# Tile order and an early merge in the routed layer of a small vision tower: expert tiles by their place within an expert, two groups' results merged beside the last tiles

## The reference, cut to what matters

```python
shared_out = _expert(x, sg, su, sd)              # silu(x @ g.T) * (x @ u.T) @ d.T, 704 hidden
probs = softmax(x @ wr.T + rb)                    # 7 routed experts
scores, idx = top_k(probs, 2)
scores = scores / scores.sum(-1, keepdims=True)
w = sum(scores[..., None] * one_hot(idx, 7), -2)
out = shared_out
for e in range(7):
    out = out + w[..., e:e+1] * _expert(x, rg[e], ru[e], rd[e])
# then block 1: layernorm, attention with 16 heads, layernorm, feed-forward
```

## Time and profile before

| | us |
|---|---|
| three runs, median (lowest to highest) | 1051.48 (1050.4 to 1051.73) |
| the profiled execution, own time | 1051.63 |
| its span, first to last instruction | 1049.8 |
| PE busy in the span | 971.6 (93%) |
| DVE, ACT, POOL busy | 709.0, 660.5, 359.1 |

### The profile page before, as it was taken

The page is one execution under the profiler, slowest core; times in us unless marked ns, Lnnn a source line. Parts: engine busy times, 40 slices in busy tenths (PEclk is TensorE's granted clock), DMA queues, the critical chain, the costliest instruction groups (busy, mean ns, idle before and its releaser), DMA issues.

```text
span 1049.8 us, 29183 instructions
## 1 busy us (share of the span) xinstructions
PE 971.6 (93%) x10745; PEld 892.2 (85%) x10746; DVE 709.0 (68%) x1393; ACT 660.5 (63%) x1206; POOL 359.1 (34%) x285
## 2 busy tenths in 40 slices
PE   4979999989999987999999999997899999799998
PEld 4967888868888886999999999996678888699998
DVE  3536677675556566899999999992566777655443
ACT  3337677855465635687777777772567678555652
POOL 0253454465665650111111111113545554611210
PEclk9999999989999998999999999999889999999999
DMA  6720000009211135111111111104311100000000
GB/s 231 240 96 3 2 3 3 3 7 357 41 35 31 40 75 221 35 36 40 35 35 40 40 35 35 40 30 141 81 26 26 26 3 4 2 13 12 24 25 24
DMA packets 30974, 57.67 MB, mean 55 GB/s; under 512 B 13202, under 2 KB 22418, under 8 KB 29724
## 3 DMA queue, kind: packets, MB, share of 16 engines
q1 hardware_dynamic: 15696, 38.38, 11.5%
q0 software_dynamic: 13664, 15.25, 4.8%
q10 hardware_dynamic: 1516, 2.65, 0.7%
HBM read 41.47 MB, written 14.67 MB: 53 GB/s over the span
## 4 chain that ended last, share of the span: by engine, by line
PE 72%; DVE 9%; ACT 9%; issue 5%; DMA 3%; POOL 1%; SPq 0%; DVEq 0%; ACTq 0%; POOLq 0%
PE ps L1400 19%; PE ps L1405 15%; PE ps L1407 14%; PE ps L1406 14%; PE ps L1805 3%; PE ps L1549 3%; PE ps L1538 2%; DVE Hd L1149 2%; DMA x_in<-in_xT_dram 2%; ACT L817 1%; ACT Hf_hi L811 1%; PE ps L1703 1%; ACT Sg L817 1%; DVE hsum L1139 1%; ACT L831 1%
## 5 line engine op out<-in xcount | busy, mean ns | idle before, releaser
L1303 DVE TENSOR_TENSOR tile_w<-arena,tile_w 128x704 fp32r<-128x704 f32 x129 | 142.7, 1134 | 26.9 <-ACT tile_w L880 24.2
L559 POOL DMA_INDIRECT routed_out<-yt,tile_to x43 | 42.1, 979 | 275.6 <-DVE yt L1321 271.5
L880 ACT ACTIVATE tile_w<-arena 128x704 fp32r x129 | 122.3, 984 | 1.4 <-issue 1.4
L1405 PE MATMUL ps<-tile_w,xTs 128*128 128x352 f32 x344 | 115.3, 335 | 4.5 <-DVE h L1276 3.0
L1406 PE MATMUL ps<-tile_w,xTs 128*128 128x352 f32 x344 | 111.6, 324 | 0.0
L1407 PE MATMUL ps<-tile_w,xTs 128*128 128x352 f32 x344 | 111.5, 324 | 0.0
L429 POOL TENSOR_TENSOR Km<-KT,cst 128x592 f32<-128x592 f32 x64 | 75.7, 1184 | 68.9 <-PE ps L1400 42.1
L1149 DVE TENSOR_TENSOR Hd<-Sg,ps 128x296 f32<-128x296 f32 x96 | 44.2, 461 | 81.2 <-ACT Sg L817 77.1
L811 ACT ACTIVATE Hf_hi<-Hd 128x296 fp32r<-128x296 f32 x96 | 43.3, 452 | 85.6 <-DVE Hd L1149 83.4
L1405 PE MATMUL ps<-xf_hi,gu_lo 128*128 128x296 f32 x272 | 85.8, 316 | 4.1 <-DVE Hd L1149 3.7
L1015 DVE SCALAR_TENSOR_TENSOR ps<-ps,bias 128x592 f32<-128x592 f32 x64 | 50.1, 782 | 53.0 <-PE ps L1400 53.0
(11 more groups left out here) (216 smaller groups left out, 3097.7 us busy)
## 6 DMA issues: line engine op xcount, KB each, us to landing
arena<-in_ew_dram SPq DMA_DIRECT2D x5, 2176.0 KB
x_in<-in_xT_dram SPq DMA_DIRECT2D x7, 888.0 KB, 5.4
xt<-routed_in SPq DMA_DIRECT2D x43, 129.0 KB, 2.0
arena<-in_ew_dram POOLq DMA_DIRECT2D x2, 2176.0 KB, 11.9
yg<-routed_out SPq DMA_DIRECT2D x8, 512.0 KB
out_dram<-h SPq DMA_DIRECT2D x8, 296.0 KB, 2.7
routed_in<-zero_x SPq DMA_DIRECT2D x12, 129.0 KB
qkv_w<-in_qkv_dram ACTq DMA_DIRECT2D x2, 768.0 KB, 6.2
```

What stands on the lines that cost most here:

```text
L880: act.activation(tile_w[half][0][:, cols], gate_up_of(w, half)[:, cols], ACT.Copy).then_inc(s.wh, 1)
L1303: dve.tensor_tensor(tile_w[half][1][:, cols], gate_up_of(w, half)[:, cols], tile_w[half][0][:, cols].bitcast(F32), ALU.subtract).then_inc( ...
L1405: pe.matmul(out_, w[1], x[0], start=start, stop=False)
```

## The change

Six things change together.

- **Tile order.** The table now puts tile k of every expert (its "level") ahead of tile k + 1 of any. It is computed on 43 partitions, one per tile, in more but narrower DVE instructions, with one PE product in the middle (`level_row`) and three that turn the columns into rows at the end. TABLE_AT spreads the pieces over chunks 0, 2, 3 and 4 (two) of group 6 and chunk 0 of group 7.
- **Early merge.** WHOLE says that the rows of group 0 are all in the first 21 tiles and those of groups 0 and 1 in the first 35. SP loads group 0 after `stored` 21 and group 1 after `stored` 35, GpSimd adds the two rows of each token between two stores, and in steps 25, 26, 39 and 40 PE transposes and DVE adds one half of the features (ADDS).
- **Norm of group 0** runs beside the last tiles: mean and variance on PE in the last step and ahead of the last down product, `cen` in DVE's last step, squares, the table switch and `lnv`, `rsd` on ACT, `xn` after DVE's last copy.
- **Weights.** The projection weights of block 1 are loaded by SP after step 40, no longer by ACT after tile 0; their lower half is computed by DVE, not by GpSimd.
- **Start of attention(1).** 8 products that nobody reads, not 22; groups 2 and 3 are loaded after the last tile; GpSimd adds group 2 after the split of group 1.
- **Start of the tiles and routing.** The table entries of tile 0 are read in chunk 3 of group 7; the first tile's transpose moves from chunk 3 to chunk 4; and DVE's `norm(r + 1)` moves from place 4 to the end of place 3.

```diff
+ADDS = {25: (0, 0), 26: (0, 1), 39: (1, 0), 40: (1, 1)}
+WHOLE = [EXPERTS * -(-(g + 1) * N // P) for g in range(2)]
...
+            t = 1
+            for adding in (25, 39):
+                with eng.Fori(0, (adding - t) // 2) as i:
+                    for k in range(2):
+                        step(2 * i + t + k, (t + k) % 2, i + (t + 1) // 2, None, False)
+                for t in range(adding, adding + 2):
+                    step(t, t % 2, (t + 1) // 2, ADDS[t], False)
+                t += 1
+            for t in range(t, TILES):
+                step(t, t % 2, (t + 1) // 2, None, t == TILES - 1)
...
+            for g, until in enumerate((24, 38)):
...
+                next_load(until, 0)
+                if g == 1:
+                    sp.wait_ge(C.mm1, FREE + 1)
+                sp.wait_ge(E.stored, FREE + WHOLE[g])
+                load_routed(g, g, yg_early)
+                next_load(until + 1, 1)
...
+            sp.wait_ge(C.mm1, FREE + 2)
+            sp.dma_start(qkv_w1, qkv1).then_inc(s_attw, 16)
+            sp.dma_start(out_w1, wo1).then_inc(s_attw, 16)
...
+                for g, until in enumerate((22, 36)):
+                    with pool.Fori(t // 2, until // 2) as i:
+                        for b in range(2):
+                            store(2 * i + b, b)
+                    sum_early(g)
+                    t = until
...
                 lower_x(a, 1, 1, xa[1])
+                if l == 1:
+                    sum_routed(2, 0, 1)
                 km(a, 0, 2)
...
                     if at == 4:
-                        if r + 1 < GROUPS:
-                            norm(r + 1)
                         slots_of(r, r % 2)
                     next(routes[r])
+                    if at == 3 and r + 1 < GROUPS:
+                        norm(r + 1)
...
+                        if l == 0 and g == GROUPS - 2 and j == 1:
+                            pe.wait_ge(s_t, TABLE_OPS[0])
+                            pe.wait_ge(s.r, RCHAIN * GROUPS)
+                            mm(ps[0:TILES, 6, 0:KT_MAX + 1], ones[0:KT_MAX, 0:TILES], level_row).then_inc(s.cnt_mm, 1)
+                        if l == 0 and g == GROUPS - 2 and j == 5:
+                            pe.wait_ge(s_t, TABLE_OPS[1])
...
-                        if l == 0 and last and j == 3:
+                        if l == 0 and last and j == 4:
                             pe.wait_ge(s.r, RCHAIN * GROUPS)
                             tile_in(0, 0, 0)
...
+                    if add:
+                        routed_out(yg_early, *add, 6)
                     hidden_t(t - 1, 1 - b)
                     gate_up_half(t, b, 1)
+                    if add:
+                        pe.wait_ge(C.h, 2 * add[0] + add[1] + 1)
                     if not last:
                         tile_in(t + 1, 1 - b, turn_next)
+                    else:
+                        mean(A[1], 0, 6)
                     tile_out(t - 1, w_before)
...
                 hidden_t(TILES - 1, 0)
+                pe.wait_ge(A[1].cen, FREE + 1)
+                variance(A[1], 0, 6)
                 tile_out(TILES - 1, weights_of(pe, TILES - 1))
...
+                over_tiles(act, step)
                 upper_down(TILES - 1)
+                squares(A[1], 0)
                 hidden_t(TILES - 1)
+                act.preload_act_table_set("natural_log_exp_and_others")
+                deviation(A[1], 0, 6)
```

More of the change, by code:

```diff
@@ L389, in _ @@
             load(0, 0)
             load(1, 1)
[L391 to L402 removed]
+            t = 2
@@ L880, in upper_weights, with step @@
                         act.activation(tile_w[half][0][:, cols], gate_up_of(w, half)[:, cols], ACT.Copy).then_inc(s.wh, 1)
-                def step(t, b, last):
+                def step(t, b, turn, add, last):
                     upper_down(t - 1)
@@ L1251, in step @@
                             routing(*routing_at(g, j))
-                        if l == 0 and g == GROUPS - 2 and j < TABLE_PIECES:
+                        if l == 0 and g == GROUPS - 2:
+                            for _ in range(TABLE_AT[j]):
+                                next(pieces)
+                        if l == 0 and last and j == 0:
                             next(pieces)
@@ L1483, in keep_going, with routed_out @@
                     mm(ps[:, 0, 0:2 * P], ident, cst[:, 0:2 * P])
+            def routed_out(of, g, c, bk):
+                pe.wait_ge(C.sum, g + 1)
+                for p in range(PAIRS):
+                    ins = pe.transpose(ps[:, bk, p * W2:(p + 1) * W2], of[:, p, 0, c * P:(c + 1) * P],
+                                       ident[0:W2, 0:W2])
+                ins.then_inc((C.mm0, C.mm1)[c], 1)
             def attention(l):
```

282 lines of the change are left out of this document (155 added, 127 removed).

## The result

| | before | after |
|---|---|---|
| runs beside each other, median (lowest to highest), us | 1050.94 (1049.59 to 1051.73, 4 runs) | 1034.80 (1031.88 to 1040.36, 4 runs) |
| the profiled execution, own time | 1051.63 | 1035.61 |
| its span | 1049.8 | 1033.8 |
| mean granted TensorE clock | 0.975 | 0.981 |

The ratio is 0.9845, 95% interval 0.9812 to 0.9878: faster by 16 us. Forecast were 1033.2 us, 8 in 10 between 1026.5 and 1042.

What follows compares the result with a forecast made beforehand. The prediction took PE's own work in the tiles and the 24 us handover into block 1 as the bound. Terms -12.7 + 2.0 - 4.5 - 3.1 = -18.3 gave 1033.2 us, 8 in 10 between 1026.5 and 1042.

Steps and rivals of the forecast that it cites:

- the likeliest case: Whole kernel: the forecast itself, terms summing to -18.3 us, 1033.2 us, own range 1030 to 1038; chance 0.52.
- The handover, -12.7: Last tile to attention(1): first projection 17 us earlier, PE standing 5 us for group 2's sum, 0.5 us half clock; -12.7 us.
- The tiles, +2.0: Tile steps: merge transposes on PE 1.5 us in all, plus 0.5 for code written out and two loops; +2.0 us.
- the sum of 2.38 is done early in step 24: Tiles: GpSimd's early sum of group 0 takes 2.38 us, in time for its use in step 25.
- Routing, -4.5: Routing: norm leaves DVE's chain (4.1 us) and PE's waits for it (6.3 us) go; -4.5 taken, between the two.
- The first rival: "Only the handover pays": routing waits pass to Hd, tile 2's rows stay late; -11.1 us, 1040.5; chance 0.18.
- The table, +0.55: Group 6 to tile 0: table wait +2.1, transpose -0.6, table entries read ahead -0.95; tile 0 starts 0.55 us late.
- Tile 2, -3.65 without what is ahead of it: Tile 2: rows land earlier without the weights' megabyte; wait -1.95, slow products -1.2 and -0.5; term -3.1 with the 0.55.
- Only the handover pays: Rival: routing waits pass to Hd and tile 2's rows stay late; -11.1 us, 1040.5; chance 0.18.
- More than the sum: Rival: waits that go take their half clock too; routing -6.5, start -4.5, handover -14.5; -24 us, 1027.5; chance 0.18.
- The handover is given back: Rival: group 2's sum waits for loads of groups 2 and 3, turn 0 stands 4 us more; 1044; chance 0.08.
- the slow GpSimd queue: Rival "slower than before": early loads over 24 us delay GpSimd's sums and stores, so tiles stand; 1055; chance 0.03.

Runs made afterwards that it cites:

- e3_hold_clock: Changed kernel plus 24 products that nobody reads on PE ahead of the merge of group 2 in turn 0; ratio 0.9858 to the kernel before.
- b3_loops_split: Kernel before, with only the tiles' steps laid out as in the change (two loops, six steps written out); 1051.65 us, one execution.
- e4_no_early_sum: Changed kernel with GpSimd's two early sums cut to 8 of 1024 elements, the rest left out of the result; ratio 0.9804 to the kernel before.
- g1_sum_halves: Changed kernel with each early sum on GpSimd cut into two halves of 128 features, a step apart; ratio 0.9827 to the kernel before.
- b1_norm_only: Kernel before, with only the routing's norm moved from place 4 to the end of place 3; 1051.58 us, one execution.
- b2_load_late: Kernel before, with only block 1's projection weight loads moved from ACT behind tile 0 to SP behind the last tile's load; 1045.79 us, one execution.
- e2_sum_dve: Changed kernel with group 2's sum moved from GpSimd to DVE, ahead of its first scores; 1030.98 us, ratio 0.9791 to the kernel before.
- e5_sum_behind: Changed kernel with group 2's sum on DVE, behind the first pair's scores chain; ratio 0.9818 to the kernel before.
- h1_all: Changed kernel with table products a chunk later, early sums halved, group 2's sum on DVE, group 3's load held for that sum; 1031.30 us, ratio 0.9809.

## Why the prediction was right, and where it was not

The sign, the size and the likeliest case came out: -18.3 was summed, -16.0 measured between the two profiled executions, and the largest term was right. That it fits to 0.1 us is luck: two errors cancel in it, and other profiles of the same code give up to 17.5.

- *The handover, -12.7.* Measured -12.6 in the first pair of profiles, -14.4 with the changed kernel's second. By the steps: the first projection was to come 17 us earlier; against T it is 37.7 and 21.3, so 16.4. PE was to stand 5 us for GpSimd's queue and stood 5.04. The table load of 1.28 has nothing behind it, which `lnv` at 713.28 shows; the drain of 1.38 us that the Trainium skill ("ScalarE: Activation LUTs", section What ACT_TABLE_LOAD costs) counts with each switch is not seen in this place either. Mis-sized was the half clock behind the stand: 0.5 said, 1.9 to 3.3 by `e3_hold_clock`. The gain of 13.2 that was to stand at the second set of scores is 12.1 there (48.07 and 35.94 behind T), and at the third set 10.2 (52.69 and 42.50). Unforeseen was that the kernel then lacks the later stretch that the one before has behind the wait at the end of turn 0 (its window from 770 is at 0.50, and 7 us at half clock cost 3.4), which brings the gain back to 12.6.
- *The tiles, +2.0.* Measured +3.2. The merges' own work was counted at 0.37 a step and is 0.22 to 0.25; the 0.5 for code and loops is 0 (`b3_loops_split`). The step that failed is "the sum of 2.38 is done early in step 24": it counted the sum as GpSimd's alone. DVE's instructions and the sum wait for each other, 0.8 us a pair (`e4_no_early_sum`, `g1_sum_halves`). The remaining 0.6 is the steps of 7.12 us, open.
- *Routing, -4.5.* Measured -5.1, but only 2.0 of it is the norm; 3 us are half clock that fell otherwise, so this too fits by luck. Neither the 4.1 of DVE's chain nor PE's 6.3 us of waits was the measure: 4.3 of the 6.3 us passed on to ACT's row copies, which the term did not count. The first rival had named such a passing on, to `Hd`, and put the whole gain at nothing.
- *The table, +0.55.* Measured +2.6 against the kernel before and +3.3 against `b1_norm_only`: this is the step that failed worst. I priced the wait in chunk 5 well (2.1, now 1.89) but not the one in chunk 1: the sum has no term for the product of `level_row`, for which PE stands 2.45 us; and the half clock behind the second wait, 3.4 us of it and so 1.7, was not counted though the earlier trace rows show such a stretch. Nor did the 0.95 for reading the table entries ahead arrive. ACT's idle time ahead of its first weight split did fall, from 1.25 to 0.46 us, but DVE's half of the split then began 1.3 us behind ACT's instead of 0.9, and PE waited 3.29 us ahead of tile 0 for 3.04.
- *Tile 2, -3.65 without what is ahead of it.* Measured -3.6, and by its named cause (`b2_load_late`, -3.1; 1.8 to 3.7 against the other kernels).
- *The rivals.* "Only the handover pays" falls with `b1_norm_only` and `b2_load_late`: in their profiles each gain is there alone, though one execution each can't show it in the time of the whole. "More than the sum" had a point in the handover, where its -14.5 is what the second profile gives, but not in routing or at the start of the tiles. "The handover is given back" and the slow GpSimd queue did not happen: the load of group 0 was issued at 565.27 and summed from 571.47, 6.2 us.

## What to carry to other kernels

When work moves to an engine that "has time", ask who shares something with it: here instructions of the two elementwise engines waited for each other, and cutting the moved piece to what the other has to spare in one step made it free. When a wait is added to a queue, list everything behind it, prefetches too: the wait for one sum on the queue of loads cost 6 us by way of weights that nobody was thinking of. When a few us are at stake and the clock moves, take two profiles of each kernel, and count the time at half clock in both before a difference is put down to a cause. And a product whose input comes from a slow chain should stand a chunk behind that chain, not at its end.

## What the runs showed of the hardware

- Some DVE instructions and GpSimd's sum run one after the other, and the one that started first is not held up. In the first profile the sum started 0.19 us behind DVE's `tile_w` and took 3.68 us. In the second it started 0.06 us ahead of it and took 2.40; it was `tile_w` that came late, 3.82 us for 1.62, ending 1.48 behind the sum, and PE waited 1.10 us for it. The sum of group 2 on DVE in `e2_sum_dve` is a third case: it began at 730.45, 0.06 us behind GpSimd's `xn` of 1.44 us, and took 2.46 instead of 1.22.

```profile
571.77 2.40 POOL L590 TENSOR_TENSOR yg_early<-yg_early 74x1024 f32<-74x1024 f32 x1 [3.21 <-DMA routed_out<-yt,tile_to]
```

```profile
571.83 3.82 DVE L1379 TENSOR_TENSOR tile_w<-arena,tile_w 128x1408 fp32r<-128x1408 f32 x1
```

```profile
575.70 0.43 PE L1489 MATMUL ps<-tile_w,xTs 128*128 128x352 f32 x1 [1.10 <-DVE tile_w L1379]
```

- Half clock follows some stands of PE and not others of the same length. The stand of 1.8 us at the end of turn 0 is followed by it in the kernel before, in `e2_sum_dve` and in `e3_hold_clock`, where no slow stretch lies in the 20 us before, and not in the changed kernel or `e5_sum_behind`, where one does. It looks as if one stretch spared the next, and in the profile of `e2_sum_dve` most of the gain went that way; but `h1_all` has a stretch from 734 to 741 and, behind the same stand, another from 751 (window from 750 at 0.61), and `b1_norm_only` and `b3_loops_split` have stretches that end 12 us ahead of the stand and again one behind it. What decides it stays open.
- A microsecond at half clock cost half a microsecond: the same code ahead of the tiles took between 110.8 and 115.0 us in nine profiles, with 2.4 to 11.3 us at half clock, and 109.3 to 109.7 with half of that taken off. A few us of a change in this kernel can be read from a stretch of the profile once that is counted, but hardly from the time of the whole.
